# A fused state-space mixer and FFN on one core: seven of a unit's eight token chunks turned by VectorE in 32x32 squares and reordered through DRAM in place of TensorE, and scaled by GpSimd

## The chip, the core and the metric

The kernel runs on one core of a Trainium2 chip. The time is the device time of one execution in microseconds, and the median over several is given. The four engines that compute are TensorE (PE in the profile, with PEld for its weight loads), VectorE (DVE), ScalarE (ACT) and GpSimd (POOL). SyncE (SP) issues nearly all the transfers.

## What is computed

The input is x, two sequences of 512 tokens with 512 channels. A projection makes, for each token, a gate and a hidden vector (128 heads of 64), B and C (8 groups of 128) and one time step dt per head. Hidden, B and C go through a causal convolution of four taps and a SiLU. Then comes a chunked scan, chunks of 128 tokens:

```python
xch = (hs * dt[..., None]).reshape(b, nc, CHUNK, H, P)          # hidden scaled by the time steps
Y_diag = einsum('bzlhn,bzshn,bhzls,bzshp->bzlhp', Cc, Bc, L, xch)   # within a chunk
states = einsum('bzlhn,bhzl,bzlhp->bzhpn', Bc, decay_states, xch)   # carried to the next chunk
Y = Y_diag + Y_off + hs * D
g = y * silu(gate)                                                # then a group norm and the output projection
```

The result is added to x and normalised, and a linear layer with folded LoRA matrices, another addition and another normalisation follow.

## The kernel before

**Tiling.** The 128 heads are 16 units of 8 heads. A group g (0 to 7) has two units, e = 0 and 1. A unit's tokens are eight chunks c of 128 (the first four are one sequence, the last four the other). One pair (g, e, c) is a step; there are 128 of them. All engines run the same order of steps, unrolled in Python, and wait for one another by semaphores. The names below are those of the code.

**Hidden values, turned.** The projection leaves the hidden values of a unit in hs with channels on partitions and tokens along the free axis (four tiles j of 128 channels). The products of a chunk need the tokens on partitions, times dt: that is xdt, 128 tokens by 8 heads by 64. Before, `front` of TensorE (line 519) turns the four 128x128 pieces of a chunk into the PSUM bank p_hid (L526), and `front` of VectorE (line 1206) multiplies p_hid by the time steps in tok into xdt (L1210).

**A step on TensorE** has, in this order: the carried part of chunk c, one tile of the projection (L514 to L516), p_yd from xdt and the decay matrix (L690), `front` of the next chunk (p_hid, and for e = 0 also p_misc, L537 and L539), the state update p_st (L700 to L702, which waits for xd_ready; not for c = 3 and 7), the output projection of the chunk before (p_out, L562 to L564, which waits for g_hi and g_lo), and the rest of the step's projection tiles.

**Projection tiles** stand in a table by step. A step has one tile (both sequences, 24 matmuls) or two or three. In e = 0 the steps c = 0, 1, 6, 7 have more than one tile, in e = 1 the steps 0, 1, 5, 6, 7.

**A step on GpSimd** (`body`, line 1083) has, in this order: for c not 0 or 4, dh + eac (L1092); for c = 1, 2, 5, 6, state times elast (L1097); the low half of a weight tile two tiles ahead, w_lo (`split_lo`, L1034); the gating of y (`gate_y`, L1144, waits for y of VectorE); now and then a small rs (L1149); `skip` of the next chunk (L1063); `decay_hidden` of the next chunk (L1052, L1054, L1056), which makes xd, xd_hi and xd_lo from xdt and lets p_st go (not for c = 3 and 7); and, in a step with more tiles, a further w_lo for each. I call the first w_lo of a step its W1 and the second its W2.

**A step on SyncE** (line 463): eac of the next chunk (waits until dh + eac is done), a decay matrix (waits for p_yd), then the weights raw of the tiles four ahead. `load_w` waits for w_lo, since raw has two buffers: in a step with two tiles, the second raw is loaded when GpSimd has done W2.

**A step on VectorE** (line 1347): three convolution taps of a sequence, y = p_yd + dh (L1375), the state (L1383 or L1385), a tap, `front` (xdt, and for e = 0 cb, b_hi, b_lo), a tap, `mix` (decay times cb, L1227), a tap, the norm's sums, g_lo (L1251), `scale_off` (eac, L1258).

```python
def front(g, e, c):                       # VectorE
    dve.wait_ge(hid_ready, step(g, e, c) + 1)
    wait(dve, xd_scaled, carried(g, e, c))
    nc.vector.tensor_tensor(xdt[:], p_hid[:], bcast(tok[:, e, 1, c, :], 2, HD), ALU.mult).then_inc(xdt_ready, 1)
```

Of the kernel before, what the change touches and what calls it, by code (L numbers as in the profile page):

```python
# [22 lines left out]
P = 128  # L23
# [11 lines left out]
EPS = 1e-5  # L35
HALVES = (slice(0, HID // 2), slice(HID // 2, HID))
# [57 lines left out]
def mixer_ffn_kernel(nc, x_t, x_tok, w_t, unit_chan, group_chan, dt_bias, a_log, wo_t,  # L94
                     ffn_w, lora_a, lora_b, lora_w, ffn_bias, eye, upper, out):
    ctx = ExitStack()
    with ctx:
# [12 lines left out]
        elast_d = nc.dram_tensor("elast_d", (HEADS, CHUNKS), F32, kind="Internal").ap()  # L110
        tok_d = nc.dram_tensor("tok_d", (P, UNITS, 3 * CHUNKS * UH), F32, kind="Internal").ap()
# [16 lines left out]
        xdt = sb("xdt", [P, UH, HD])  # L128
        xd = sb("xd", [P, UH, HD])
# [51 lines left out]
        hid_ready, xdt_ready, xd_ready = sem("hid_ready"), sem("xdt_ready"), sem("xd_ready")  # L181
        cb_ready, cb_taken, bhi_ready = sem("cb_ready"), sem("cb_taken"), sem("bhi_ready")
# [74 lines left out]
        def decay_round(g, e, c):  # L257

            return 8 * g + (4 * e + c // 2 + 1) if c % 2 else 4 * g + (2 * e + c // 4 + 1)

# [119 lines left out]
        def _(sp):  # L380
            def load_w(g, t):
# [79 lines left out]
            sp.wait_ge(tok_here, 1)  # L461

            def body(g, last):
                for e in range(2):
                    for c in range(8):
# [34 lines left out]
        def _(pe):  # L500
# [528 lines left out]
        def _(pool):  # L1029
# [14 lines left out]

            def decay_hidden(g, e, c):
# [32 lines left out]
            pool.wait_ge(tok_here, 1)  # L1078
            decay_hidden(0, 0, 0)
# [3 lines left out]
            def body(g, last):  # L1083
                for e in range(2):
                    for c in range(8):
# [15 lines left out]
                        for i, t in enumerate(tiles):  # L1101
# [3 lines left out]
                            if i == 0 and (g, e, c) == (0, 0, 0):  # L1105
                                decay_hidden(0, 0, 1)
# [431 lines left out]
```

## Time and profile before

| | |
|---|---|
| median of 3 runs | 1598.37 us (1598.18 to 1598.73) |
| span of the profiled execution | 1596.2 us; what lies around the span, against the median, is 2.2 us |
| TensorE busy | 1577.7 us, 99% |
| VectorE busy | 1347.6 us, 84% |
| ScalarE busy | 1230.8 us, 77% |
| GpSimd busy | 1224.1 us, 77% |
| TensorE's granted clock | 9 (90% of full speed or more) in each of 40 slices |
| DMA | 178.69 MB, 34% of the 16 engines' span |

The profile is of one execution. The profiled execution's own time is its span, 1596.2 us, and the 2.2 us around it. Matmuls overlap in the records: a matmul lasts longer than the distance to the next, so what one costs is read from the distance between starts. PEld is the weight load, which overlaps too. "Idle before" is the engine's wait ahead of an instruction, with what ended it.

### The profile page before, as it was taken

The page shows a single profiled execution, that of the slowest core. Times are in us where ns is not written, and L with a number is a line of the kernel's source. Part 1 is how long each engine was busy: PE and PEld are TensorE (multiplying, and loading weights), DVE is VectorE, ACT ScalarE, POOL GpSimd, SP SyncE. Part 2 cuts the span into 40 slices and gives each one's busy share as a digit, 9 for nine tenths or more (in the row PEclk, how much of TensorE's full clock was granted, in tenths as well). Part 3 has the DMA queues.
Part 4 walks back from the last instruction along what each step waited for, and adds up shares of the span by engine and source line. Part 5 has one row for each costly group of instructions (what it writes and reads, how often), then busy time and mean ns, then how long its engine had stood idle before and what let it go on. Part 6 is the DMA issues. An engine that isn't in the chain of part 4 may idle for free.

```text
span 1596.2 us, 27397 instructions
## 1 busy us (share of the span) xinstructions
PE 1577.7 (99%) x9112; PEld 1299.6 (81%) x9112; DVE 1347.6 (84%) x1878; ACT 1230.8 (77%) x2391; POOL 1224.1 (77%) x1013
## 2 busy tenths in 40 slices
PE   8999999999999999999999999999999999999998
PEld 6878888888888888888888888888888888888865
DVE  6787898879979799787988889887998879978797
ACT  5888778886778877787877877878777886878864
POOL 4578788787797868878687787878688786787864
PEclk9999999999999999999999999999999999999999
DMA  3643424233242322333234332433334333342411
GB/s 116 200 157 108 130 83 153 87 115 108 87 145 96 123 100 100 129 100 109 87 115 140 99 123 74 131 118 92 116 101 136 102 102 106 100 149 77 142 60 60
DMA packets 88156, 178.69 MB, mean 112 GB/s; under 512 B 16592, under 2 KB 20688, under 8 KB 87760
## 3 DMA queue, kind: packets, MB, share of 16 engines
q1 hardware_dynamic: 87008, 176.77, 34.2%
q8 instruction: 74, 1.21, 0.3%
q14 instruction: 66, 0.54, 0.1%
q10 hardware_dynamic: 1008, 0.17, 0.1%
HBM read 172.17 MB, written 4.72 MB: 111 GB/s over the span
## 4 chain that ended last, share of the span: by engine, by line
PE 94%; DVE 1%; POOL 1%; ACT 1%; issue 1%; DMA 0%; SPq 0%; POOLq 0%; DVEq 0%; ACTq 0%
PE proj L514 16%; PE proj L516 16%; PE proj L515 16%; PE p_yd L690 8%; PE p_out L562 7%; PE p_out L564 7%; PE p_out L563 7%; PE p_st L571 5%; PE p_hid L526 4%; PE proj L626 2%; PE p_st L702 1%; PE p_st L700 1%; PE p_st L701 1%; PE p_misc L537 1%; PE p_misc L583 0%
## 5 line engine op out<-in xcount | busy, mean ns | idle before, releaser
L514 PE MATMUL proj<-x_hi,w_hi 128*128 128x512 f32 x1160 | 462.0, 398 | 7.6 <-DVE x_lo L1323 7.0
L515 PE MATMUL proj<-x_lo,w_hi 128*128 128x512 f32 x1160 | 452.9, 390 | 0.0
L516 PE MATMUL proj<-x_hi,w_lo 128*128 128x512 f32 x1160 | 452.9, 390 | 0.0
L1034 POOL TENSOR_TENSOR w_lo<-raw,w_hi 128x512 fp32r<-128x512 f32 x209 | 284.2, 1364 | 101.8 <-ACT w_hi L754 99.3
L1198 DVE SCALAR_TENSOR_TENSOR hs<-proj,uch,hs 128x511 f32<-128x511 f32 (+2 forms) x384 | 285.4, 743 | 42.4 <-ACT hs L781 37.5
L842 ACT ACTIVATE decay<-decay,tok 128x128 f32<-128x128 f32 x1024 | 312.4, 391 | 0.0
L514 PEld LDWEIGHTS proj<-x_hi,w_hi 128*128 128x128 f32 x1160 | 218.8, 189 | 53.2 <-issue 11.2
L516 PEld LDWEIGHTS proj<-x_hi,w_lo 128*128 128x128 f32 x1160 | 218.3, 188 | 46.2
L515 PEld LDWEIGHTS proj<-x_lo,w_hi 128*128 128x128 f32 x1160 | 218.9, 189 | 42.2
L1227 DVE TENSOR_TENSOR decay<-decay,cb 128x1024 f32<-128x1024 f32 x128 | 199.0, 1555 | 56.0 <-ACT decay L860 54.3
L1092 POOL TENSOR_TENSOR dh<-dh,eac 128x512 f32<-128x512 f32 x96 | 127.2, 1325 | 144.0 <-DVE eac L1258 140.3
L1144 POOL TENSOR_TENSOR y<-y,gate 128x512 f32<-128x512 f32 x128 | 180.0, 1406 | 50.3 <-DVE y L1375 50.3
L562 PE MATMUL p_out<-wo_hi,g_hi 128*128 128x512 f32 x512 | 203.6, 398 | 3.3 <-DVE g_lo L1251 3.3
L564 PE MATMUL p_out<-wo_hi,g_lo 128*128 128x512 f32 x512 | 200.1, 391 | 0.0
L563 PE MATMUL p_out<-wo_lo,g_hi 128*128 128x512 f32 x512 | 199.5, 390 | 0.0
L781 ACT ACTIVATE hs<-proj,uch 128x512 f32<-128x512 f32 x128 | 98.6, 773 | 78.8 <-PE proj L516 77.9
L980 ACT ACTIVATE ysq<-y 128x512 f32<-128x512 f32 x128 | 79.9, 624 | 98.8 <-POOL y L1144 98.8
L1375 DVE TENSOR_TENSOR y<-p_yd,dh 128x512 f32<-128x512 f32 x128 | 87.7, 685 | 68.7 <-PE p_yd L690 41.5
L1063 POOL TENSOR_TENSOR dh<-hs,uch 128x512 f32<-128x512 f32 x122 | 145.1, 1189 | 0.0
L754 ACT ACTIVATE w_hi<-raw 128x512 fp32r<-128x512 f32 x197 | 122.8, 623 | 28.2 <-PE proj L516 28.2
L1056 POOL TENSOR_TENSOR xd_lo<-xd,xd_hi 128x512 fp32r<-128x512 f32 x96 | 135.9, 1416 | 7.7
L690 PE MATMUL p_yd<-decay,xdt 128*64 128x128 f32 x2048 | 140.1, 279 | 0.0
(139 smaller groups left out, 3037.6 us busy)
## 6 DMA issues: line engine op xcount, KB each, us to landing
decay<-acum_d SPq DMA_DIRECT2D x128, 512.0 KB, 4.4
raw<-w_t SPq DMA_DIRECT2D x209, 256.0 KB, 2.9
eac<-eacum_d SPq DMA_DIRECT2D x192, 128.0 KB, 3.0
wo_raw<-wo_t SPq DMA_DIRECT2D x32, 256.0 KB, 4.0
c_new<-wo_t SPq DMA_DIRECT2D x32, 256.0 KB, 4.2
hs<-x_t SPq DMA_DIRECT2D x8, 256.0 KB, 5.7
acc<-x_tok SPq DMA_DIRECT2D x8, 256.0 KB, 3.1
out<-acc SPq DMA_DIRECT2D x8, 256.0 KB, 2.0
```

Of the source, the lines that this page charges most:

```text
L514: nc.tensor.matmul(dst[:], w_hi[:, ws, k, :], x_hi[:, k, cols], start=(k == 0), stop=False)
L515: nc.tensor.matmul(dst[:], w_hi[:, ws, k, :], x_lo[:, k, cols], start=False, stop=False)
L516: mm = nc.tensor.matmul(dst[:], w_lo[:, ws, k, :], x_hi[:, k, cols], start=False, stop=(k == KC - 1))
L562: nc.tensor.matmul(p_out[:], g_hi[:, j, :], wo_hi[:, j, :], start=(j == 0), stop=False)
L563: nc.tensor.matmul(p_out[:], g_hi[:, j, :], wo_lo[:, j, :], start=False, stop=False)
L564: mm = nc.tensor.matmul(p_out[:], g_lo[:, j, :], wo_hi[:, j, :], start=False, stop=(j == UT - 1))
L690: mm = nc.tensor.matmul(p_yd[(h % 2) * HD:(h % 2 + 1) * HD, h // 2, :], xdt[:, h, :], decay[:, dslot(c), h, :], start=True, stop=True)
L842: ins = nc.scalar.activation(decay[:, dslot(c), h, :], decay[:, dslot(c), h, :], ACT.Relu, scale=-1.0, bias=tok[:, e, 0, c, h:h + 1])
L1034: nc.gpsimd.tensor_tensor(w_lo[:, s].rearrange("p a b -> p (a b)"), raw[:, s, :], w_hi[:, s].rearrange("p a b -> p (a b)").bitcast(F32), A ...
L1144: nc.gpsimd.tensor_tensor(y[:], y[:], gate[:, c // CPB, :, (c % CPB) * P:(c % CPB + 1) * P], ALU.mult).then_inc(gated, 1)
L1198: nc.vector.scalar_tensor_tensor(out=dst[:, shift:], in0=src[:, :SEQ - shift], scalar=w, in1=dst[:, shift:], op0=ALU.mult, op1=ALU.add).th ...
L1227: nc.vector.tensor_tensor(decay[:, dslot(c)], decay[:, dslot(c)], bcast(cb[:, c, :], 1, UH), ALU.mult).then_inc(mix_ready, 1)
```

## The change

For the chunks c = 1 to 7 of every unit the turning leaves TensorE. Chunk 0 stays as it was. For the others:

1. VectorE's new `turn_blocks` transposes a chunk's hidden values in 32x32 squares, hs to x_blk (one instruction, 128x512). It does so two chunks ahead, in the place where `front` had multiplied.
2. SyncE's `store_blocks` writes x_blk to DRAM (turned_d), one transfer of 256 KB; `load_blocks`, behind the weights of the step, waits until that has landed and reads it back in four transfers of 64 KB, each to 32 partitions in runs of 512 bytes, to x_tok_sb. Now tokens lie on partitions.
3. GpSimd's `scale_tokens` multiplies x_tok_sb by dt_blk into xdt, behind W1 and ahead of `gate_y`, when x_here says that the four reads have landed and p_yd of the running chunk is done. `lay_dt` copies a unit's time steps to dt_blk, two small copies per unit.

The scratch for GpSimd's own DMA descriptors is made smaller to leave room for the new tiles; GpSimd issues no transfers.

```diff
@@ SyncE
+            def store_blocks(g, e, c):
+                n = turn_n(g, e, c)
+                sp.wait_ge(blocks_turned, n)
+                wait(sp, x_here, 64 * (n - 2))
+                sp.dma_start(turned_d[n % 2].rearrange("i a n -> (i a) n"),
+                             x_blk[:].rearrange("p q j b -> p (q j b)")).then_inc(blocks_stored, 16)
+            def load_blocks(g, e, c):
+                n = turn_n(g, e, c)
+                sp.wait_ge(blocks_stored, 16 * n)
+                wait(sp, x_here, 64 * (n - 1))
+                wait(sp, xdt_ready, step(g, e, c) - 1)
+                for q in range(UT):
+                    sp.dma_start(x_tok_sb[q * BLK:(q + 1) * BLK, n % 2].rearrange("a i j b -> a i (j b)"),
+                                 turned_d[n % 2, :, :, q * P:(q + 1) * P].rearrange("i a n -> a i n")).then_inc(x_here, 16)
...
+                        o2, e2, c2 = ahead(e, c, 2)
+                        if c2 and not (last and o2):
+                            store_blocks(g + o2, e2, c2)
                         for t in tiles_of(e, c, last):
                             off, n = divmod(t.n + 4, GRP_TILES)
                             if not (last and off):
                                 load_tile(g + off, LOOP_TILES[n], last)
+                        if c2 and not (last and o2):
+                            load_blocks(g + o2, e2, c2)
@@ TensorE, front
-                wait(pe, xdt_ready, step(g, e, c))
-                if c == 0 or c == CPB:
-                    pe.wait_ge(hs_ready, 8 * u + (8 if c else 7 if u else 4))
-                for j in range(UT):
-                    mm = nc.tensor.transpose(p_hid[:, 2 * j:2 * j + 2, :].rearrange("p a b -> p (a b)"),
-                                             hs[:, e, j, c * P:(c + 1) * P], ident[:])
-                mm.then_inc(hid_ready, 1)
+                if c == 0:
...
@@ GpSimd
+            def scale_tokens(g, e, c):
+                pool.wait_ge(x_here, 64 * turn_n(g, e, c))
+                pool.wait_ge(yd_ready, step(g, e, c))
+                if c == 1:
+                    pool.wait_ge(dt_blk_ready, 2 * (2 * g + e + 1))
+                nc.gpsimd.tensor_tensor(xdt[:].rearrange("p h d -> p (h d)").rearrange("p (j i b) -> p i j b", j=UT, i=UT),
+                                        x_tok_sb[:, turn_n(g, e, c) % 2], bcast(dt_blk[:, c], 3, BLK), ALU.mult).then_inc(xdt_ready, 1)
...
                             elif i == 0:
+                                if c < 7:
+                                    scale_tokens(g, e, c + 1)
                                 gate_y(g, e, c)
@@ VectorE
+            def turn_blocks(g, e, c):
+                u = 2 * g + e
+                wait(dve, blocks_stored, 16 * (turn_n(g, e, c) - 1))
+                dve.wait_ge(hs_ready, 8 * u + (8 if c >= CPB else 7 if u else 4))
+                nc.vector.transpose(x_blk[:], hs[:, e, :, c * P:(c + 1) * P].rearrange("p j (q a) -> p q j a", q=UT)
+                                    ).then_inc(blocks_turned, 1)
...
                         if more:
                             front(g + off, ne, ncn)
+                        o2, e2, c2 = ahead(e, c, 2)
+                        if c2 and not (last and o2):
+                            turn_blocks(g + o2, e2, c2)
```

GpSimd's rows from the end of step (e = 1, c = 7) of a group through step (e = 0, c = 0) of the next, before:

```order
L1034 TENSOR_TENSOR w_lo<-raw,w_hi 128x512 x2
L1144 TENSOR_TENSOR y<-y,gate 128x512
L1149 TENSOR_TENSOR rs<-var,minus_half 128x1
L1063 TENSOR_TENSOR dh<-hs,uch 128x512
L1052 TENSOR_TENSOR xd<-xdt,tok 128x512
L1054 CAST xd_hi<-xd 128x512
L1056 TENSOR_TENSOR xd_lo<-xd,xd_hi 128x512
L1034 TENSOR_TENSOR w_lo<-raw,w_hi 128x512
```

and the same place after the change, where the first w_lo is W2 of step 7, the second W1 of step 0 and the last W2 of step 0:

```order
L1069 TENSOR_TENSOR w_lo<-raw,w_hi 128x512
L1087 COPY dt_blk<-tok 128x16x4
L1087 COPY dt_blk<-tok 128x16x4
L1069 TENSOR_TENSOR w_lo<-raw,w_hi 128x512
L1095 TENSOR_TENSOR xdt<-x_tok_sb,dt_blk 128x4x4x32
L1205 TENSOR_TENSOR y<-y,gate 128x512
L1210 TENSOR_TENSOR rs<-var,minus_half 128x1
L1116 TENSOR_TENSOR dh<-hs,uch 128x512
L1105 TENSOR_TENSOR xd<-xdt,tok 128x512
L1107 CAST xd_hi<-xd 128x512
L1109 TENSOR_TENSOR xd_lo<-xd,xd_hi 128x512
L1069 TENSOR_TENSOR w_lo<-raw,w_hi 128x512
```

The scaling now stands between W1 and the gating, ahead of all else that the step makes. SyncE's rows from step (e = 0, c = 7) to the first of step (e = 1, c = 1), before:

```order
L366 DMA decay<-acum_d 128x1024
L388 DMA raw<-w_t 128x512 x2
L355 DMA uch<-unit_chan 128x28
L345 DMA tok<-tok_d 128x192
L351 DMA elast<-elast_d 128x64
L374 DMA eac<-eacum_d 64x512 x2
L366 DMA decay<-acum_d 128x1024
L388 DMA raw<-w_t 128x512 x2
L374 DMA eac<-eacum_d 64x512 x2
```

and after:

```order
L376 DMA decay<-acum_d 128x1024
L396 DMA turned_d<-x_blk 128x512
L416 DMA raw<-w_t 128x512 x2
L406 DMA x_tok_sb<-turned_d 32x4x128 x4
L365 DMA uch<-unit_chan 128x28
L355 DMA tok<-tok_d 128x192
L361 DMA elast<-elast_d 128x64
L384 DMA eac<-eacum_d 64x512 x2
L376 DMA decay<-acum_d 128x1024
L396 DMA turned_d<-x_blk 128x512
L416 DMA raw<-w_t 128x512 x2
L406 DMA x_tok_sb<-turned_d 32x4x128 x4
```

The four reads of x_tok_sb stand behind the second raw, and so behind the wait for W2 that raw has.

## Rows read from the trace of the kernel before

**Rows 1.** The page, busy time, share of the span and instructions of engines.

```profile
PE 1577.7 (99%) x9112; PEld 1299.6 (81%) x9112; DVE 1347.6 (84%) x1878; ACT 1230.8 (77%) x2391; POOL 1224.1 (77%) x1013
```

**Rows 2.** The page, the chain of work that ended last, shares by line.

```profile
PE proj L514 16%; PE proj L516 16%; PE proj L515 16%; PE p_yd L690 8%; PE p_out L562 7%; PE p_out L564 7%; PE p_out L563 7%; PE p_st L571 5%; PE p_hid L526 4%; PE proj L626 2%; PE p_st L702 1%; PE p_st L700 1%; PE p_st L701 1%; PE p_misc L537 1%; PE p_misc L583 0%
```

**Rows 3.** Timeline of TensorE, start and length, behind two p_yd (e = 0, e = 1).

```profile
709.91 0.66 PE L526 MATMUL p_hid<-ident,hs 128*128 128x128 f32 x4
710.41 0.39 PE L537 MATMUL p_misc<-cT,bT 128*128 128x128 f32 x2
710.55 0.47 PE L700 MATMUL p_st<-xd_hi,b_hi 128*128 128x512 f32 x1
...
730.32 1.09 PE L690 MATMUL p_yd<-decay,xdt 128*64 128x128 f32 x16
731.35 0.66 PE L526 MATMUL p_hid<-ident,hs 128*128 128x128 f32 x4
731.76 0.48 PE L700 MATMUL p_st<-xd_hi,b_hi 128*128 128x512 f32 x1
```

**Rows 4.** Groups by line: count, busy us, mean ns, idle before and its releasers.

```profile
L1052 POOL TENSOR_TENSOR xd<-xdt,tok 128x512 f32<-128x512 f32 x96 | 135.0, 1406 | 0.6 <-DVE xdt L1210 0.6
L1210 DVE TENSOR_TENSOR xdt<-p_hid,tok 128x512 f32<-128x512 f32 x128 | 87.1, 680 | 0.0
```

**Rows 5.** The tile xdt: shortest, median and longest ns, first and last start.

```profile
L1052 POOL TENSOR_TENSOR xd<-xdt,tok x96: 1036/1087/2047, 65.1 to 1550.1; 128x512 f32<-128x512 f32 x96
```

**Rows 6.** Timeline of GpSimd, (e = 1, c = 7) into the next group's first step.

```profile
831.05 2.52 POOL L1034 TENSOR_TENSOR w_lo<-raw,w_hi 128x512 fp32r<-128x512 f32 x2
833.53 1.29 POOL L1144 TENSOR_TENSOR y<-y,gate 128x512 f32<-128x512 f32 x1
...
838.98 1.29 POOL L1056 TENSOR_TENSOR xd_lo<-xd,xd_hi 128x512 fp32r<-128x512 f32 x1
```

**Rows 7.** Timeline of SyncE's queue, start and length of issues.

```profile
832.39 0.33 SPq L388 DMA_DIRECT2D raw<-w_t  x1
...
843.24 1.09 SPq L374 DMA_DIRECT2D eac<-eacum_d  x2
```

**Rows 8.** DMA issues: count, KB each, median us from issue to landing.

```profile
eac<-eacum_d SPq DMA_DIRECT2D x192, 128.0 KB, 3.0
...
tok<-tok_d SPq DMA_DIRECT2D x14, 96.0 KB, 2.6
```

**Rows 9.** Timeline of TensorE, first step of a group and the second step's update.

```profile
830.74 1.09 PE L690 MATMUL p_yd<-decay,xdt 128*64 128x128 f32 x16
...
844.35 0.48 PE L700 MATMUL p_st<-xd_hi,b_hi 128*128 128x512 f32 x1
```

**Rows 10.** Timeline of GpSimd at other steps: (0,1) into (0,2), (0,6), (1,0).

```profile
649.72 1.66 POOL L1034 TENSOR_TENSOR w_lo<-raw,w_hi 128x512 fp32r<-128x512 f32 x1
...
657.70 1.30 POOL L1144 TENSOR_TENSOR y<-y,gate 128x512 f32<-128x512 f32 x1 [1.89 <-DVE y L1375]
...
663.26 1.69 POOL L1056 TENSOR_TENSOR xd_lo<-xd,xd_hi 128x512 fp32r<-128x512 f32 x1
...
707.86 1.31 POOL L1056 TENSOR_TENSOR xd_lo<-xd,xd_hi 128x512 fp32r<-128x512 f32 x1
...
730.96 2.54 POOL L1034 TENSOR_TENSOR w_lo<-raw,w_hi 128x512 fp32r<-128x512 f32 x2
...
738.38 1.30 POOL L1056 TENSOR_TENSOR xd_lo<-xd,xd_hi 128x512 fp32r<-128x512 f32 x1
```

**Rows 11.** Timeline of TensorE, state updates of steps (0,2) and (1,1).

```profile
668.07 0.47 PE L700 MATMUL p_st<-xd_hi,b_hi 128*128 128x512 f32 x1
...
743.15 0.48 PE L700 MATMUL p_st<-xd_hi,b_hi 128*128 128x512 f32 x1
```

More of the change, by code:

```diff
@@ L110, in mixer_ffn_kernel @@
         elast_d = nc.dram_tensor("elast_d", (HEADS, CHUNKS), F32, kind="Internal").ap()
+        turned_d = nc.dram_tensor("turned_d", (2, UT, BLK, UT * P), F32, kind="Internal").ap()
         tok_d = nc.dram_tensor("tok_d", (P, UNITS, 3 * CHUNKS * UH), F32, kind="Internal").ap()
@@ L128, in mixer_ffn_kernel @@
         xdt = sb("xdt", [P, UH, HD])
+        x_blk = sb("x_blk", [P, UT, UT, BLK])
+        x_tok_sb = sb("x_tok_sb", [P, 2, UT, UT, BLK])
+        dt_blk = sb("dt_blk", [P, CHUNKS, UT, UT])
         xd = sb("xd", [P, UH, HD])
@@ L461, in _ @@
             sp.wait_ge(tok_here, 1)
+            store_blocks(0, 0, 1)
+            load_blocks(0, 0, 1)
             def body(g, last):
@@ L521, in front @@
                 u = 2 * g + e
-                wait(pe, xdt_ready, step(g, e, c))
-                if c == 0 or c == CPB:
-                    pe.wait_ge(hs_ready, 8 * u + (8 if c else 7 if u else 4))
-                for j in range(UT):
-                    mm = nc.tensor.transpose(p_hid[:, 2 * j:2 * j + 2, :].rearrange("p a b -> p (a b)"),
-                                             hs[:, e, j, c * P:(c + 1) * P], ident[:])
-                mm.then_inc(hid_ready, 1)
+                if c == 0:
+                    wait(pe, xdt_ready, step(g, e, c))
+                    pe.wait_ge(hs_ready, 8 * u + (7 if u else 4))
+                    for j in range(UT):
+                        mm = nc.tensor.transpose(p_hid[:, 2 * j:2 * j + 2, :].rearrange("p a b -> p (a b)"),
+                                                 hs[:, e, j, c * P:(c + 1) * P], ident[:])
+                    mm.then_inc(hid_ready, 1)
                 if e == 0:
@@ L1043, in split_both, with lay_dt @@
                 split_lo(g, t)
+            def lay_dt(u):
+                g, e = u // 2, u % 2
+                if g:
+                    pool.wait_ge(unit_loaded[e], 48 * g + 32)
+                wait(pool, xdt_ready, 8 * u)
+                for r in range(2):
+                    nc.gpsimd.tensor_copy(dt_blk[:, :, r::2, :], tok[:, e, 1].rearrange("p c (j q) -> p c q j", j=UT)).then_inc(dt_blk_ready, 1)
+            def scale_tokens(g, e, c):
[5 more added lines that the diff above has]
+                                        x_tok_sb[:, turn_n(g, e, c) % 2], bcast(dt_blk[:, c], 3, BLK), ALU.mult).then_inc(xdt_ready, 1)
             def decay_hidden(g, e, c):
@@ L1117, in body @@
                         if not tiles:
[L1118 removed]
+                            if c < 7:
+                                scale_tokens(g, e, c + 1)
+                            else:
                                 lagged_rms(g, e, c)
@@ L1126, in body @@
                                     skip(g + off, ne, ncn)
+                        if c == 7 and not (last and off):
+                            lay_dt(2 * g + e + 1)
                         if last and e == 1 and c >= 5:
@@ L1206, in front @@
             def front(g, e, c):
-                dve.wait_ge(hid_ready, step(g, e, c) + 1)
-                wait(dve, xd_scaled, carried(g, e, c))
-                nc.vector.tensor_tensor(xdt[:], p_hid[:], bcast(tok[:, e, 1, c, :], 2, HD), ALU.mult).then_inc(xdt_ready, 1)
+                if c == 0:
+                    dve.wait_ge(hid_ready, 2 * g + e + 1)
+                    wait(dve, xd_scaled, carried(g, e, c))
+                    nc.vector.tensor_tensor(xdt[:], p_hid[:], bcast(tok[:, e, 1, c, :], 2, HD), ALU.mult).then_inc(xdt_ready, 1)
                 if e == 0:
```

10 lines of the change are left out of this document (8 added, 2 removed).

## The prediction

> **What bounds the kernel now.** I read the page's busy times first: TensorE is busy 99% of the span, GpSimd 77%, VectorE 84% [rows 1]. The chain that ended last says the same: nearly all of it is TensorE's own lines, and p_hid, the turning, has 4% [rows 2]. So a matmul that leaves shortens the kernel, as long as the other engines still deliver before TensorE asks. The second reading is therefore how early they deliver. In the timeline I set the end of GpSimd's xd_lo, which is what the state update p_st waits for, against the start of p_st:
>
> - chunk 1 of e = 0: 838.98 + 1.29 = 840.27 against 844.35, slack 4.1 [rows 6, 9];
> - chunk 1 of e = 1: 739.68 against 743.15, slack 3.5 [rows 10, 11];
> - chunk 2 of e = 0: 664.95 against 668.07, slack 3.1 [rows 10, 11];
> - chunk 6 of e = 0: 709.17 against 710.55, slack 1.4 [rows 3, 10].
>
> These are margins of 1.4 to 4.1 us in steps of some 12 (1596.2/128). GpSimd idles 23% on average, but not there.
>
> **What TensorE gives back.** p_hid to the next matmul is 710.41 - 709.91 = 0.50 us for e = 0 and 731.76 - 731.35 = 0.41 for e = 1 [rows 3]; I take it that what follows p_yd now starts where p_hid did. 56 chunks of each kind leave: 56 x 0.50 + 56 x 0.41 = 51.0 us. The floor is 1598.4 - 51.0 = 1547.4.
>
> The Trainium skill (TensorE: Matmul & The Clock Gate, Part 4) gives about 275 ns for a transpose on TensorE within a kernel. By that 448 of them would be 123 us and the time 1475. The rows decide against it: the records last that long, but they start 0.10 to 0.125 us apart, so the 51.0 stands.
>
> **VectorE.** 112 products of 0.68 us leave [rows 4] and 112 transposes of the same 512 elements per partition come, in the same place. No row has such a transpose. Bounds: the 0.68 of the product, and twice that; I take 0.68 as the same element count, so nothing. Twice would add 0.7 us to steps in which VectorE is nearly full, at most 112 x 0.7 = 76 us if all showed; I reckon a quarter, 19.
>
> **GpSimd** gets 112 products. Nearest row: xd<-xdt,tok, also 512 elements with a broadcast operand, 1036 ns at the shortest, 1406 in the mean, 2047 at the longest [rows 4, 5]. I take 1.2. Its load goes from 1224 to 1224 + 134 = 1358 us, 85% of the old span: it still fits on average. dt_blk's 32 small copies I cost at nothing: they stand where GpSimd waits for ScalarE or a step's first weights.
>
> The spread from 1036 to 2047 for one instruction shows contention [rows 5]. The Trainium skill (SBUF — State Buffer, two separate sides) says that GpSimd and a VectorE operation with two SBUF inputs exclude each other at a shared port pair for the whole instruction. It speaks against the change, since p_hid lay in PSUM and the new product reads and writes SBUF only. By it the longest value would be common, and 112 x (2.05 - 1.2) = 95 us more GpSimd time would result; the mean in the rows above lies far nearer the short end.
>
> **The round trip through DRAM.** The reads of x_tok_sb stand in SyncE's queue behind the second raw of a step, and that waits for GpSimd's W2 (in the rows: W2 ends at 831.05 + 1.26 = 832.31, raw is issued at 832.39) [rows 6, 7]. From the end of W2: raw 0.35, four issues at about 0.5 each (two eac took 1.09 [rows 7]), of which three lie ahead of the last one's start, and the last one's landing. For that the neighbours are 2.6 (96 KB) and 3.0 (128 KB) [rows 8]; I take 2.75. T = 0.35 + 1.5 + 2.75 = 4.6 us. Bounds: 3.9 (issues of 0.33, landing 2.6) and 5.3 (issues of 0.55, landing 3.3 behind raw's own 256 KB). In steps with one tile nothing holds the reads: turned some 5 us behind p_yd, stored (up to 3.0) and read (4.3), they land some 12 us behind p_yd, and the product wants them 13 behind it or later. There I cost the trip at nothing; its cover is about 1 us.
>
> With two tiles there is a loop: W2 of step c-1, T, the product for c+1 in step c, then gating, skip, decay_hidden, W2 of step c, and again T. Behind the product in GpSimd's queue stand the gating (which ScalarE's squares and g_hi and VectorE's g_lo wait for) and decay_hidden (which p_st waits for).
>
> **Chunk 1 of e = 0.** Product from 832.31 + 4.6 = 836.9, gating from 838.1 in place of 833.53: 4.6 late [rows 6]. The slack is 4.1, and TensorE arrives 2 x 0.50 earlier. p_st waits 4.6 - 4.1 + 1.0 = 1.5 us.
>
> **Chunk 1 of e = 1.** W2 ends at 730.96 + 1.27 = 732.2, the product starts at 736.8, the gating at 738.0 in place of 733.5: 4.5 late; with the slack of 3.5 and 2 x 0.41: 1.9 us [rows 10, 11].
>
> **Chunk 2 of e = 0.** W2 of step 0 ended at 649.72 + 1.66 = 651.38, the gating began 6.3 later, after a wait of 1.89 for y [rows 10]. Now W2 is 4.6 late, the gating can follow 4.6 + 1.2 = 5.8 behind it: 4.1 late in all. Slack 3.1; TensorE has gained 3 x 0.50 and lost 1.5: 1.0 us. I add 1.0 for chunk 4, to which the lateness passes by the squares and eac on VectorE; this is an estimate from chunk 2's.
>
> **Chunk 6 of e = 0 and chunk 4 of e = 1**, the tight ones in plain steps: slack 1.4, product 1.04 (part of it in a wait for y), TensorE 1.0 earlier: 0.7 us each. I read the second's slack as 6's.
>
> **The start.** The first product has no earlier unit to hide under, and pays store and read: 3 us more, an estimate from T.
>
> **The sum.** Waits: 8 x 1.5 + 8 x 1.9 + 8 x (1.0 + 1.0) + 15 x 0.7 + 3 = 12 + 15.2 + 16 + 10.5 + 3 = 56.7. Against 51.0: +5.7. The profiled execution, 1596.2 + 2.2 around it, is the median's 1598.4; so 1604.
>
> **Rivals.**
> *The round trip is shorter or better hidden: faster.* For: with T = 3.9 each of the four looped places (chunks 1, 1, 2, 4) loses about 0.7 of its wait, 8 x 4 x 0.7 = 22: 1582. Should the product fall into waits for y in the tight steps, as one of 1.89 us shows [rows 10], another 10 go: 1572. It decides where T is below about 4.4 (5.7/32 = 0.2 under my value). Against: four issues with a raw of 256 KB ahead of them. Chance 0.28 for 1555 to 1595.
> *All is hidden.* 1547. For: GpSimd has 372 us of idle time [rows 1]. Against: the slacks above. 0.08.
> *The trip or contention is worse.* T = 5.3: +22, 1626; twice the transpose: +19, 1623; both 1645. For: VectorE and GpSimd would both be near 90% in H steps. 0.30 for above 1614.
> *It only changes places, as forecast:* waits of p_st for xd_lo eat what TensorE gave back, 1595 to 1614. 0.34.
> That the change doesn't take p_hid off TensorE is excluded by the order of its instructions.
>
> **How the numbers follow.** 1604 is the forecast of the likeliest case. Two runs of this kernel differ by up to 0.03%, and about 0.2% (3.2 us) is what a measurement can tell from no change. Faster by over that: 0.08 + 0.28; of the likeliest case's 0.34, 0.12 lies within 0.2% of 1598.4 and 0.22 above it; so slower is 0.22 + 0.30 = 0.52. The range leaves out full success and the sum of all the bad bounds: 1565 to 1640. The likeliest case's own range is 1595 to 1614.
>
> **What would show it.** TensorE: 64 p_hid instead of 512, its busy time some 50 us lower, and its idle time up from 18 to some 75 us, the largest part "p_st waits for GpSimd's xd_lo" with 1 to 2 us at chunks 1 of both units, little at chunks 3 and 7. GpSimd: a wait ahead of the product, released by the DMA to x_tok_sb, of 3 us in steps (0,0) and (1,0), under 1 in one-tile steps. x_tok_sb from W2's end to landing: 4.6. VectorE: the transpose at 0.6 to 0.7, its idle time unchanged. The product at 1.0 to 1.4. The prediction is wrong if x_tok_sb lands within 3.5 us of W2, if the product waits in one-tile steps as well (the cover of 1 us is thin: 0.5 us in each of the 8 such steps of a group would be 30 us), if the transpose takes over 1 us, or if waits move to p_yd or p_out through g_lo.

## The result and the profile after

The changed kernel takes 1672.19 us (median of 4 runs, 1671.84 to 1673.55) against 1598.46 of the kernel before on the same chip: ratio 1.0464, interval 1.045 to 1.0479. It is 73.7 us slower. The forecast had 1604, range 1565 to 1640.

The page of the changed kernel: busy times, then the chain that ended last by engine, then some groups of instructions (busy, mean ns | idle before, releaser), then the new transfers (KB each, us to landing).

```profile
PE 1567.9 (94%) x8664; PEld 1268.2 (76%) x8664; DVE 1380.4 (83%) x1878; ACT 1230.5 (74%) x2391; POOL 1376.6 (82%) x1157
...
POOL 31%; PE 21%; issue 19%; DVE 16%; ACT 8%; DMA 2%; SPq 2%; ACTq 0%; DVEq 0%; POOLq 0%
...
L1015 ACT ACTIVATE ysq<-y 128x512 f32<-128x512 f32 x128 | 80.6, 630 | 221.0 <-POOL y L1205 220.9
...
L1095 POOL TENSOR_TENSOR xdt<-x_tok_sb,dt_blk 128x512 f32<-128x512 f32 x112 | 123.1, 1099 | 61.8 <-DMA x_tok_sb<-turned_d 61.8
...
turned_d<-x_blk SPq DMA_DIRECT2D x112, 256.0 KB, 2.5
x_tok_sb<-turned_d SPq DMA_DIRECT2D x448, 64.0 KB, 2.1
```

Against [rows 1]: TensorE does 448 matmuls less, yet its busy time falls by only 9.8 us (1577.7 to 1567.9), and span less busy time grows from 18.5 to 103.8. The chain, nearly all TensorE before [rows 2], now runs a third over GpSimd. The granted clock, its mean over the span:

```profile
core 0: 1671.7 us, clock 0.986
```

It was 0.999 in the run before; 0.013 of 1671.7 is 21.7 us.

What TensorE waits for, in the view of waits (us in total, times, longest). Before, this view had 0.4 us of p_st for xd_lo, 0.6 of proj for "issue", and none for var.

```profile
PE p_st L735 <- POOL xd_lo L1109: 31.7, 30, 2.2
PE p_misc L572 <- DVE var L1309: 20.1, 12, 2.3
PE proj L549 <- issue: 15.2, 18, 1.9
PE proj L549 <- DVE x_lo L1393: 6.9, 1, 6.9
PE p_hid L561 <- ACT hs L828: 4.5, 5, 1.5
PE p_out L597 <- issue: 4.4, 7, 0.8
PE p_st L735 <- DVE eac L1328: 3.4, 1, 3.4
```

**One trip, followed.** GpSimd's timeline from the end of step (0,7) to step (1,1) of a group (start, length, [idle before]):

```profile
961.14 1.74 POOL L1069 TENSOR_TENSOR w_lo<-raw,w_hi 128x512 fp32r<-128x512 f32 x1
962.83 0.41 POOL L1087 COPY dt_blk<-tok 128x64 f32<-128x64 f32 x2
963.20 1.29 POOL L1069 TENSOR_TENSOR w_lo<-raw,w_hi 128x512 fp32r<-128x512 f32 x1
967.04 1.74 POOL L1095 TENSOR_TENSOR xdt<-x_tok_sb,dt_blk 128x512 f32<-128x512 f32 x1 [2.55 <-DMA x_tok_sb<-turned_d]
968.75 1.28 POOL L1205 TENSOR_TENSOR y<-y,gate 128x512 f32<-128x512 f32 x1
...
972.84 1.59 POOL L1109 TENSOR_TENSOR xd_lo<-xd,xd_hi 128x512 fp32r<-128x512 f32 x1
974.40 1.72 POOL L1069 TENSOR_TENSOR w_lo<-raw,w_hi 128x512 fp32r<-128x512 f32 x1
976.08 1.75 POOL L1146 TENSOR_TENSOR dh<-dh,eac 128x512 f32<-128x512 f32 x1
977.78 1.51 POOL L1151 TENSOR_TENSOR state<-state,elast 128x512 f32<-128x512 f32 x1
979.25 1.72 POOL L1069 TENSOR_TENSOR w_lo<-raw,w_hi 128x512 fp32r<-128x512 f32 x1
```

SyncE's queue at the same place:

```profile
962.95 0.33 SPq L416 DMA_DIRECT2D raw<-w_t  x1
963.39 1.79 SPq L406 DMA_DIRECT2D x_tok_sb<-turned_d  x4
```

And TensorE's timeline:

```profile
971.68 1.09 PE L725 MATMUL p_yd<-decay,xdt 128*64 128x128 f32 x16
974.49 0.50 PE L735 MATMUL p_st<-xd_hi,b_hi 128*128 128x512 f32 x1 [1.71 <-POOL xd_lo L1109]
...
976.22 0.47 PE L549 MATMUL proj<-x_hi,w_hi 128*128 128x512 f32 x1 [0.77 <-issue]
976.52 0.39 PE L550 MATMUL proj<-x_lo,w_hi 128*128 128x512 f32 x1
...
981.07 0.65 PE L549 MATMUL proj<-x_hi,w_hi 128*128 128x512 f32 x1 [1.85 <-issue]
981.52 0.63 PE L550 MATMUL proj<-x_lo,w_hi 128*128 128x512 f32 x1
981.94 0.63 PE L551 MATMUL proj<-x_hi,w_lo 128*128 128x512 f32 x1
```

W2 of step 7 ends at 962.88 (961.14 + 1.74), and the second raw and the four reads are issued at once; only when the last has landed can the product start, at 967.04, 4.2 later. The gating follows at 968.75, 5.9 behind W2's end, where before it followed 1.2 behind [rows 6]. TensorE then waits three times: for xd_lo (1.71), for the low half w_lo that is ready at 976.12 (0.77), and for the next at 980.97 (1.85). The view calls the last two "issue", since the wait lies at the weight load; both end 0.10 behind GpSimd's w_lo, as do all of this name at this step. Behind the third gap matmuls of 512 columns start 0.43 apart, not 0.23. The granted clock of that stretch (windows: us, TensorE busy, matmuls, granted clock, DMA share, GB/s):

```profile
976.00:980.00 4.00, 3.00 (x12) 1.00 0.51 132
980.00:984.00 4.00, 2.93 (x7) 0.65 0.85 261
984.00:988.00 4.00, 4.00 (x18) 0.92 0.20 70
```

So TensorE fell from its upper level (2.4 GHz) to the lower (1.2 GHz) for some 3.4 us (by these shares from 981.2 to 984.6), in which eight matmuls took 0.2 us more each, 1.6 in all.

Not every fall costs that. The profiled execution has this step in seven groups with such waits. In two the fall came behind the third gap, and the step took 25.8 us. In three it came ahead of the third gap, which shrank from 1.85 to 0.28, 0.28 and 1.00, and the step took 24.2. In two there was no fall, though the third gap was 1.88 and 1.85, and the step took 23.6 and 24.4. A fall ahead of a wait was paid by the wait.

**The other late chain** is at the step (0,1) of a group, on VectorE:

```profile
878.25 1.11 DVE L1497 TENSOR_REDUCE sqs<-ysq 128x128 f32<-128x512 f32 x1 [2.84 <-ACT ysq L1015]
879.28 1.34 DVE L1321 TENSOR_TENSOR g_lo<-y,g_hi 128x512 fp32r<-128x512 f32 x1
...
881.74 1.24 DVE L1315 SCALAR_TENSOR_TENSOR wo_lo<-wo_raw,uch,wo_hi 128x512 fp32r<-128x512 f32 x1
882.90 0.15 DVE L1309 TENSOR_SCALAR var<-p_misc 128x1 f32<-128x1 f32 x1
```

and TensorE at the same place:

```profile
879.79 1.09 PE L725 MATMUL p_yd<-decay,xdt 128*64 128x128 f32 x16
883.20 0.46 PE L572 MATMUL p_misc<-cT,bT 128*128 128x128 f32 x2 [2.31 <-DVE var L1309]
```

The late gating makes the squares (ysq) late; VectorE stands idle 2.84 us before its sum of them; var, which it reads out of p_misc, stands behind that; and `front` of TensorE may not write p_misc before.

### The profile page after: what moved, and what is told of

It reads as the page before. It is cut to its first block, busy times and chain, and to the rows that moved or that the text cites. A ratio compares the mean times of both kernels' runs of the same rounds, so it can differ in the third digit from the quotient of the medians.

```text
span 1671.7 us, 27534 instructions
## 1 busy us (share of the span) xinstructions
PE 1567.9 (94%) x8664; PEld 1268.2 (76%) x8664; DVE 1380.4 (83%) x1878; ACT 1230.5 (74%) x2391; POOL 1376.6 (82%) x1157
## 4 chain that ended last, share of the span: by engine, by line
POOL 31%; PE 21%; issue 19%; DVE 16%; ACT 8%; DMA 2%; SPq 2%; ACTq 0%; DVEq 0%; POOLq 0%
POOL y L1205 7%; DVE hs L1259 5%; PE proj L549 5%; PE proj L550 5%; PE proj L551 5%; POOL w_lo L1069 4%; POOL xd L1105 4%; POOL dh L1116 3%; POOL xd_lo L1109 3%; POOL xdt L1095 3%; POOL dh L1146 2%; DVE g_lo L1321 2%; ACT decay L877 2%; POOL xd_hi L1107 2%; DMA x_tok_sb<-turned_d 2%
## 5 line engine op out<-in xcount | busy, mean ns | idle before, releaser
L549 PE MATMUL proj<-x_hi,w_hi 128*128 128x512 f32 x1160 | 467.1, 403 | 22.1 <-issue 15.2
L1069 POOL TENSOR_TENSOR w_lo<-raw,w_hi 128x512 fp32r<-128x512 f32 x209 | 293.1, 1404 | 36.2 <-ACT w_hi L789 31.4
L549 PEld LDWEIGHTS proj<-x_hi,w_hi 128*128 128x128 f32 x1160 | 221.4, 191 | 73.7 <-issue 30.7
L1146 POOL TENSOR_TENSOR dh<-dh,eac 128x512 f32<-128x512 f32 x96 | 131.1, 1366 | 111.1 <-DVE eac L1328 111.0
L597 PE MATMUL p_out<-wo_hi,g_hi 128*128 128x512 f32 x512 | 208.0, 406 | 9.2 <-issue 4.4
L1205 POOL TENSOR_TENSOR y<-y,gate 128x512 f32<-128x512 f32 x128 | 194.9, 1522 | 11.0 <-DVE y L1446 11.0
L1095 POOL TENSOR_TENSOR xdt<-x_tok_sb,dt_blk 128x512 f32<-128x512 f32 x112 | 123.1, 1099 | 61.8 <-DMA x_tok_sb<-turned_d 61.8
L1116 POOL TENSOR_TENSOR dh<-hs,uch 128x512 f32<-128x512 f32 x122 | 155.8, 1277 | 0.0
```

The lines of the kernel that those rows point to most:

```text
L549: nc.tensor.matmul(dst[:], w_hi[:, ws, k, :], x_hi[:, k, cols], start=(k == 0), stop=False)
L597: nc.tensor.matmul(p_out[:], g_hi[:, j, :], wo_hi[:, j, :], start=(j == 0), stop=False)
L1069: nc.gpsimd.tensor_tensor(w_lo[:, s].rearrange("p a b -> p (a b)"), raw[:, s, :], w_hi[:, s].rearrange("p a b -> p (a b)").bitcast(F32), A ...
L1116: nc.gpsimd.tensor_tensor(dh[:], hs[:, e, :, c * P:(c + 1) * P], bcast(d_skip(e), 2, P), ALU.mult).then_inc(dskip_done if c % CPB else dh_ ...
L1205: nc.gpsimd.tensor_tensor(y[:], y[:], gate[:, c // CPB, :, (c % CPB) * P:(c % CPB + 1) * P], ALU.mult).then_inc(gated, 1)
```

## The experiments

All are 4 runs each beside the kernel before on the same chip (1598.0 to 1598.4). "Idle" is span less TensorE's busy time: 18.5 us before, 103.8 in the changed kernel. Step times are medians over the groups of p_yd to p_yd, from starts in the timeline. Where a run lies outside the ranges that were expected of it, the text says so.

**e1: TensorE's turning taken away, nothing put in.** The kernel before; TensorE turns chunk 0 alone, VectorE multiplies an old p_hid.

```diff
-                wait(pe, xdt_ready, step(g, e, c))
-                ... four transposes, every chunk
+                if c == 0:
+                    ... wait and four transposes
-                dve.wait_ge(hid_ready, step(g, e, c) + 1)
+                dve.wait_ge(hid_ready, 2 * g + e + 1)
```

> The kernel before, in which TensorE turns only chunk 0 of a unit; for chunks 1 to 7 VectorE multiplies what chunk 0 left in p_hid, so the turning of seven chunks is left out and nothing takes its place. It shows what the removal gives by itself. Both theories (GpSimd's added work is what costs; the wait for the round trip through DRAM is what costs) need about the same: the sum of the steps that kept their pace in the changed kernel says 0.40 us for each of 112 chunks, 45 us, so 1553; by the 0.41 and 0.50 of the prediction 1547. Above 1565 the removal itself opens gaps, and part of the miss would be there.

Measured 1587.99 (ratio 0.994, 0.9923 to 0.9956), 23 us above the 1565 from which the removal itself opens gaps. Its busy times and two of TensorE's waits:

```profile
PE 1541.0 (97%) x8664; PEld 1256.1 (79%) x8664; DVE 1348.5 (85%) x1878; ACT 1228.1 (77%) x2391; POOL 1225.3 (77%) x1013
...
PE p_st L700 <- DVE eac L1258: 7.8, 9, 1.2
...
PE p_misc L537 <- DVE var L1239: 5.9, 6, 1.0
```

Busy 1541.0 is 36.7 less than before, not 51; idle is 44.7, 26 more. Steps such as (0,2) shorten by 0.39 (11.63 to 11.23), but (0,1) grows by 0.6, (0,6) by 0.65 and (1,4) by 0.7, with waits for VectorE's eac, var and state. **With the other engines' work as it was, 10 us were to be had.**

**e2: the changed kernel without store and load**, a constant in x_tok_sb, so the seven chunks' values are left out.

```diff
-                            store_blocks(g + o2, e2, c2)
...
-                            load_blocks(g + o2, e2, c2)
...
-                pool.wait_ge(x_here, 64 * turn_n(g, e, c))
```

> The changed kernel without store_blocks and load_blocks: VectorE still transposes, GpSimd still multiplies, but a constant tile that is filled once, and it waits only for p_yd of the chunk before. Left out: the real hidden values of seven chunks. If GpSimd's added work (112 products of 1.1 us, ahead of the gating, and what queues behind them) costs the time, it stays slow: 1625 to 1660. If the wait for the round trip (61.8 us ahead of the products in all) and what it shifts costs it, this comes close to the removal alone: 1555 to 1580. In between, both.

**e3: the load put behind the first raw of a step with several tiles**, everything else as changed.

```diff
-                        for t in tiles_of(e, c, last):
+                        for i, t in enumerate(tiles_of(e, c, last)):
+                            if i == 1 and c2 and not (last and o2):
+                                load_blocks(g + o2, e2, c2)
...
-                        if c2 and not (last and o2):
+                        if len(tiles_of(e, c, last)) < 2 and c2 and not (last and o2):
                             load_blocks(g + o2, e2, c2)
```

> The changed kernel with one move on SyncE: in steps with two or three tiles the four reads of x_tok_sb are issued behind the first weights' transfer, no longer behind the second, which waits for GpSimd's second w_lo. Theory of the round trip: the waits of 2.5 us at chunk 0 and about 1 at chunk 1 vanish and with them most of the loss, 1600 to 1625. Theory of GpSimd's work: at most 62 us of waits go and the work moves up into them, but the queue stays full in these steps, 1640 to 1665.

e2: 1611.80 (1.0084, 1.0069 to 1.0099), between its two ranges, so both causes count. e3: 1615.58 (1.0113, 1.0098 to 1.0128), in the range of the round trip. The profile of e3, busy times and GpSimd's wait for the trip:

```profile
PE 1551.6 (96%) x8664; PEld 1259.8 (78%) x8664; DVE 1393.7 (86%) x1878; ACT 1227.7 (76%) x2391; POOL 1380.3 (85%) x1157
...
POOL xdt L1097 <- DMA x_tok_sb<-turned_d: 7.2, 3, 4.0
```

One move of the load takes GpSimd's wait from 61.8 to 7.2 us and the time down by 56.6. What the transfers cost otherwise, contention for the DMA engines too, is within e3 less e2: 3.8 us.

**e4: the kernel before with an unused product of 128x512 on GpSimd** at the change's place, 112 times (smaller descriptor scratch, to make room).

```diff
+                                if c < 7:
+                                    scale_tokens(g, e, c + 1)     # x_tok_sb times dt_blk, to an unused tile
                                 gate_y(g, e, c)
```

> The kernel before with one thing added: GpSimd's product of 128x512, from and to tiles that nobody else uses, at the place where the change puts it (behind the first w_lo of a step, ahead of the gating, 112 times, behind p_yd of the chunk before). TensorE keeps its turning and VectorE its product. Theory of GpSimd's work: the time rises by 30 to 70 us, to 1630 to 1670, with waits of TensorE at steps (1,1), (0,1) and (1,7). Theory of the round trip: under 15 us, below 1613.

1621.90 (1.0149, 1.0134 to 1.0165), clock 1.0, between its two ranges: 23.8 us over the kernel before. 10 of them are idle (28.8). The other 13 are TensorE's busy time; half of them, 6.4 us, lies within p_out, whose matmuls start 0.233 apart in place of 0.227. In e2, e3, e12 and the changed kernel, which have the same product, they start 0.227 apart, so these 6.4 us can't be put down to the product alone; the cause of the 13 stays open. What this run shows of the product is the 10 us of idle time.

**e5: e2 with the product on VectorE; e6: e3 with the product on VectorE; e7: the changed kernel with the product behind the gating; e8: e3 with it there.**

```diff
e5, e6, front of VectorE
+                else:
...
+                    nc.vector.tensor_tensor(xdt[:]..., x_tok_sb[:, turn_n(g, e, c) % 2], bcast(dt_blk[:, c], 3, BLK), ALU.mult)
e7, e8, GpSimd
-                                if c < 7:
-                                    scale_tokens(g, e, c + 1)
                                 gate_y(g, e, c)
+                                if c < 7:
+                                    scale_tokens(g, e, c + 1)
```

> This is e2 (no store, no load, a constant in x_tok_sb) with the product by the time steps moved back to VectorE, at the place that its product has in the kernel before: GpSimd's work is again that of the kernel before but for the laying out of the time steps, and VectorE has the turn in squares (0.70 us, 112 times) beside its product. It leaves out the values of the seven chunks. Theory A, GpSimd's 123 us of products are what stands between e2 and e1 (1611.8 and 1588.0): 1588 to 1594, with POOL y again waiting for VectorE some 40 to 50 us in sum. Theory B, VectorE's 79 us of turning cost it (VectorE holds y, the variance and g_lo back): 1604 to 1616, no better than e2.

> This is e3 (in steps with more than one tile the load of the turned blocks stands behind the first weight load) with the product on VectorE as in e5; it computes everything. If what is left of the trip is hidden (in e3 the blocks land before their use almost everywhere) and GpSimd's products are the other half, it lies within 4 us of e5, 1588 to 1598, perhaps ahead of the kernel before. If the trip still comes late in some steps, VectorE waits for x_tok_sb at the head of its queue, and y and the squares with it: 1610 to 1630, no better than e3's 1615.6. If VectorE's added work decides, e5 and e6 both stand at 1604 to 1616.

> This is the changed kernel with one difference in GpSimd's order: the product stands behind the gating of y rather than ahead of it. The load is as late as in the changed kernel. If the wait for the round trip does its harm through the queue, because the gating stands behind it and with it the squares, the variance and p_misc, then the waits of p_misc for the variance at (0,1) and (1,7) (some 20 us in all) and the late ysq go, while xd_lo comes no later, since the product now fills the time that the trip takes: 1640 to 1655. If instead xd_lo and w_lo are what TensorE waits for and the gating's own wait for y is merely put ahead of them, it is unchanged or slower: 1668 to 1690.

> This is e3 with the product behind the gating of y: early load, later product. If e3's remaining loss of some 17 us over the kernel before is the gating held back by the product (1.1 us of GpSimd's time ahead of it in each step), it gains 5 to 15 us: 1600 to 1611. If it is GpSimd's sum of work, or xd_lo and w_lo at the end of its step, the order does not matter or hurts: 1613 to 1630.

e5: 1621.10 (1.0144, 1.0126 to 1.0161). e6: 1625.54 (1.0174, 1.0157 to 1.0191). e7: 1655.44 (1.0359, 1.0344 to 1.0375). e8: 1631.44 (1.0208, 1.0193 to 1.0223). Theory A of e5 was wrong, relieving GpSimd cost 9 us more than it gave, and e5 lies above theory B's range too. e6 falls in the range of a trip that still comes late, but not for that reason: VectorE waits for x_tok_sb once, 6.4 us. e7 and e8 are 0.4 and 1.4 us over the ranges whose side they take. A part of e5's loss is the product's length on VectorE; in the tile's view (shortest/median/longest ns) the same 512 elements from SBUF and from PSUM:

```profile
L1259 DVE TENSOR_TENSOR xdt<-x_tok_sb,dt_blk x112: 680/1207/1847, 70.4 to 1584.3; 128x512 f32<-128x512 f32 x112
L1253 DVE TENSOR_TENSOR xdt<-p_hid,tok x16: 678/680/682, 63.8 to 1506.7; 128x512 f32<-128x512 f32 x16
```

e7 bore the queue out: with the same late load, the gating freed from the product is worth 16.8 us; (1,7) falls from 13.51 to 11.69 and (0,1) from 16.76 to 15.66, and p_misc waits 11.3 us for var in place of 20.1. With the early load (e8 against e3) the same move costs 15.9, by later xd_lo at (1,4) and later eac at (1,5). So the product belongs ahead of the gating once its data are there in time.

**e9: e3 with the laying out of the time steps in step (e,0); e10: e9 with squares for ten of sixteen chunks only.**

```diff
e9, scale_tokens
                 if c == 1:
+                    if (g, e) != (0, 0):
+                        lay_dt(2 * g + e)
...
-                        if c == 7 and not (last and off):
-                            lay_dt(2 * g + e + 1)
e10
+IN_SQUARES = ((1, 3, 4, 5, 6), (1, 3, 4, 6, 7))
...
```

> This is e3 with GpSimd's laying out of the time steps (two copies, once a unit) moved from step (e,7) to step (e,0), just ahead of the first product of the unit; it computes everything. If these copies are what keeps the variance back at the end of a unit, the step (1,7) falls from e3's 11.73 us towards e1's 10.28 and the kernel by up to 10 us, to 1605 to 1610. If the delay at (1,7) is the products ahead of it in the queue, it stays at 11.7 and the kernel at 1612 to 1618.

> This is e9 with TensorE turning chunks 0, 2, 7 of the first unit and 0, 2, 5 of the second unit of a pair of units, and the squares the other ten: GpSimd then has no product in steps (0,1), (0,6), (1,1) and (1,4), where e3 lost. It computes everything. If the loss is made by the product in those steps, they come back to what e1 shows and the kernel to 1588 to 1596, level with or just ahead of the kernel before (1598). If VectorE, GpSimd and ScalarE are behind over a whole unit, and those steps are only where TensorE meets them, the waits appear again there or one step on, and the time is 1600 to 1612.

e9: 1627.04 (1.018, 1.0165 to 1.0195), its (1,7) unchanged at 11.73: the copies were not the cause. But it is 11.5 us slower than e3, above both ranges. Of the 7.1 us between the two profiled executions 5.2 are at (1,1), where the last gap is now 1.86 or 1.87 in all of groups 1 to 6, and the granted clock falls behind five of them, against three in e3. e10: 1621.69 (1.0148, 1.0133 to 1.0164), above both ranges as well. Both hopes fell. In e10 the waits moved on, to (1,5) (10.7 us for eac). That fits engines which are behind over the whole unit, but isn't shown: in the step before, VectorE has a product and a turn, as it has throughout e11 below, whose (1,5) is as long (15.38 for 15.40; 13.92 in e3).

**e11: e1 with VectorE's turn alone; e12: e2 without it, GpSimd's product alone.** With e1 and e2 they make a table.

```diff
e11, VectorE
+                        if c2 and not (last and o2):
+                            turn_blocks(g + o2, e2, c2)      # result unused
e12, VectorE: the same lines taken away
```

> This is e1 (TensorE turns chunk 0 alone, VectorE's product as before from an old p_hid) with VectorE's turn in squares added at the changed kernel's place, its result unused; nothing is stored or loaded, GpSimd is untouched. It leaves out the right values of seven chunks. It prices VectorE's 0.70 us, 112 times, by itself on e1's 1588.0. Theory A, VectorE has room: 1588 to 1592. Theory B, VectorE sets TensorE's pace at (0,1), (0,6) and (1,7): 1598 to 1615, and then most of e5's 1621 is VectorE's.

> This is e2 (no store, no load, constant in x_tok_sb) without VectorE's turn in squares: GpSimd has its 112 products and the laying out of the time steps, VectorE 76 us less than in the kernel before. It leaves out the values of seven chunks. With e1, e2 and e11 it makes a table of both engines' added work. Theory A, GpSimd's product costs what it adds: 1605 to 1612, nearly e2. Theory B, each engine's work alone is nearly hidden and only both together cost: 1588 to 1597.

| | time | idle | clock |
|---|---|---|---|
| e1, neither | 1587.99 | 44.7 | 0.999 |
| e11, VectorE's turn (and its product) | 1608.98 | 65.1 | 0.999 |
| e12, GpSimd's product | 1623.81 | 65.1 | 0.992 |
| e2, both (VectorE's product gone) | 1611.80 | 62.2 | 0.999 |

Ratios to before: e11 1.0068 (1.0053 to 1.0083), in theory B's range; e12 1.0157 (1.0141 to 1.0174), above both of its ranges. Either engine's added work makes TensorE idle 20 us more, and both together no more than one. e5 is e11 with the product's inputs in SBUF and the laying out on GpSimd: VectorE is busy 39 us more and the time 12.1 longer. But e12, with 80 us less work on VectorE than e2, is 12.0 us slower at nearly the same idle time. Their timelines at the step (1,1) differ by 0.2 us of a gap: 1.65 to 1.67 us in e2 and no fall of the clock behind any of the six; 1.85 to 1.88 in e12, and a fall behind five of six. In e3 both occur: 1.66 or 1.67 three times without, 1.85 or 1.86 three times with a fall. (The expectation of e14 puts a fall in every pair of units; it was five.) These are single executions: e2's profiled one has the clock of the table, its others 0.996 to 0.999, e12's 0.992 to 0.996. e12 itself prices a fall: the step took 21.98 us in the group without one and 23.54 to 23.59 in the five with, so 1.6 each, 8 in all. The longer gap at the same clock makes it 21.98 for 21.55, 0.4 each. e2, timeline and window (us, busy time and count of TensorE, PEld, VectorE, ScalarE and GpSimd, granted clock, DMA share, GB/s):

```profile
751.39 0.47 PE L543 MATMUL proj<-x_hi,w_hi 128*128 128x512 f32 x1 [1.67 <-issue]
...
752.00:756.00 4.00, 4.00 (x19) 3.30 (x18) 4.00 (x5) 1.64 (x3) 4.00 (x4) 1.00 0.36 126
```

e12:

```profile
756.13 0.47 PE L543 MATMUL proj<-x_hi,w_hi 128*128 128x512 f32 x1 [1.86 <-issue]
...
757.14 0.60 PE L544 MATMUL proj<-x_lo,w_hi 128*128 128x512 f32 x1
757.53 0.63 PE L545 MATMUL proj<-x_hi,w_lo 128*128 128x512 f32 x1
...
756.00:760.00 4.00, 3.87 (x11) 3.17 (x12) 2.17 (x3) 0.71 (x2) 4.00 (x4) 0.64 0.51 176
```

**e13, e14: the gaps of step (1,1) filled** in the changed kernel and in e12, with 84 unused matmuls into p_hid.

```diff
+                        if (e, c) == (1, 1) and not last:
+                            fill(4)                        # ahead of p_st
...
+                                if e == 1 and not last:
+                                    fill(4)                # ahead of each projection behind p_st
                                 project(g, t)
```

> This is the changed kernel with unused matmuls of 512 columns (0.23 us each at full clock) on TensorE in step (1,1): four ahead of the state update p_st and four ahead of each projection tile that follows it, where TensorE waits 1.7, 0.8 and 1.9 us in the changed kernel; it computes everything. Theory A, the fall of the granted clock behind these gaps is a cost of its own: where it fell at (1,1) the projections that follow go at full clock again, the granted clock of the run rises from 0.986 to 0.989 or more, and the time falls by 5 to 15 us, to 1657 to 1667. Theory B, the gaps alone are the cost, and the matmuls only take time: 1672 to 1690, as the filling cannot fit exactly.

> This is e12 (GpSimd's product alone, no trip, no turns; 1623.8 us, granted clock 0.992, a fall of the clock behind the gap of step (1,1) in every pair of units) with the same unused matmuls as e13. It leaves out the values of seven chunks. Theory A: the falls at (1,1) go, the granted clock is 0.998 or more, the step (1,1) goes from 23.5 us to the 21.6 of e2, and the time to 1609 to 1615, which is e2's, so that e12 and e2 differ by the clock alone. Theory B: the falls stay or the filling costs what it saves, 1622 to 1632, and the 12 us between e12 and e2 have another cause.

e13: 1667.76 (1.0435, 1.0419 to 1.0451), clock 0.991, 0.8 us over theory A's range. e14: 1617.31 (1.0116, 1.0099 to 1.0133), clock 0.997, between its two ranges; the step (1,1) goes from 23.54 to 22.01, without a fall in any group that was filled. The page of e14:

```profile
PE 1565.0 (97%) x8748; PEld 1273.9 (79%) x8748; DVE 1318.6 (82%) x1766; ACT 1226.1 (76%) x2391; POOL 1387.0 (86%) x1158
```

**More work, less time:** 84 matmuls of 0.23 us, 19 us of TensorE's time, and the kernels are 4.4 and 6.5 us faster. The falls behind these gaps are a cost of their own. e14 is what shows it: by steps, 7.0 us of the profiled execution's gain are at (1,1). e13 is weaker: only 3.5 us of its profiled gain are at (1,1), 3.8 are at (0,4), which was not filled, and the other steps lose on balance. e14 stays 5.5 over e2, so I can't say that the clock explains all 12.0, but it explains at least 6.5.

## Why the prediction was wrong, by its steps

It said slower as the likelier sign, and the wait for the trip that it named is the largest part; the size missed the range by 32 us, and most of the path from that wait to TensorE was another. By steps of one run to the next: before 1598.2, turning gone -10.2 (e1), both engines' work +23.8 (e2), transfers with an early load +3.8 (e3), the load behind the second raw +56.6 (after). In the profiled execution idle rose by 85.3 and busy time fell by 9.8, 75.5 in sum; the forecast had 56.7 and 51.0, 5.7 in sum. So 28.6 of the miss are in the waits and 41.2 in what TensorE gave back.

**Right.** *The trip.* From W2's end to the product in (0,0) and (1,0) it took 4.1 to 5.7 us, 4.2 in the median of 15, against T = 4.6; the pieces were raw 0.33, four issues 1.79 in all (0.45 each for 0.5) and a median landing of 2.1 for 2.75. GpSimd's wait of 61.8 lies as forecast at (0,0) and (1,0), 43.6 of it, 2.7 a time for 3; but it also waited 0.6 a time in a one-tile step, (0,2), hardly in the others, and 1.1 a time at (1,6) in seven groups. The prediction had named waits in one-tile steps as a sign against it.

*The transpose* took 0.70 for 0.68, *the product* 1.10 for 1.2 (1042 ns at the shortest, 1052 in the median, 2058 at the longest). The Trainium skill (SBUF — State Buffer, two separate sides) has GpSimd and a VectorE operation with two SBUF inputs exclude each other at a shared port pair; that did not make the longest value common on GpSimd, and what there is of it shows on VectorE's side, in e5. The prediction's bound for a doubled transpose, 112 x 0.7, is 78 and not 76, which changes nothing.

*Four of the six places where p_st was to wait*, summed from TensorE's idle rows by step: (1,1) 14.9 for 15.2 (11.5 for xd_lo in seven groups, 3.4 for eac in the last), (0,4) 7.4 for 8, (0,6) and (1,4) together 10.5 for 10.5. How well these sums agree is in part luck: the 8 of (0,4) was carried over from chunk 2, where nothing came of it, and in e1, without any trip or product, p_st at (0,6) waits 6.9 all the same, for eac.

**Wrong, the waits: 56.7 forecast, 85.3 measured.** The step that failed is "T, then p_st": I followed the lateness only to xd_lo, which is 31.7 of the 85.3. But all that stands behind the product in GpSimd's queue is late by as much. At (0,1) p_st was to wait 1.5 us a time, 12 in all; it waited 2.2 in all, since TensorE was stopped ahead of it in `front`, by var: 8.6 there and 11.4 at (1,7). At (0,2), where 8 were forecast, p_st never waited for xd_lo, since TensorE came later from (0,1). At (1,1) the projections waited 13.8 for w_lo, on top of p_st. p_hid waited 4.5 at (1,7) for hs. The prediction named p_yd and p_out through g_lo as places that would prove it wrong; it did not look at p_misc, though the gating's lateness was in its sum.

**Wrong, what TensorE gives back: 51.0 forecast.** The term is too large, and it is not what the time gets. Steps without a wait shorten by 0.37 to 0.41 in e1, 112 x 0.39 = 44; its busy time falls by 36.7 and its time by 10.2 only, since VectorE's and GpSimd's chain was as near as TensorE's. The slacks of 1.4 to 4.1 us were read at four places; at (0,1) p_misc for var and at (0,6) p_st for eac, which set much of e1, I had read none. So the floor of 1547 and the rival "all is hidden" were never there: 1588 is what is left with no new work at all. And the rival of a shorter trip (1555 to 1595) had no room either: with no trip whatever, e2 takes 1611.8.

**Wrong, left out: the clock.** Busy time fell by 9.8 where e1's fell by 36.7: 26.9 us of longer matmuls, 21.7 of them by the mean granted clock (0.986 for 0.999). The lower level came behind gaps, and the work that followed paid. e14 shows that it can be a cost of its own. The 21.7 are worked out from the clock and are busy time; what they cost directly is less, since at (1,1) three of the five falls were paid by shorter waits. e13 got back 4.4; the rest of the clock's share is not shown by a run.

**The rivals.** "The trip or contention is worse" (1623 to 1645) had the right sign and the wrong reason: T was 4.2 and not 5.3, and the transpose was not doubled. "GpSimd's load still fits on average" (85% forecast) was right as a sum and beside the point: in e4 the product alone makes TensorE idle 10 us more. Of the 152.5 us that GpSimd's busy time rose, 123.1 are the products, 6.6 the laying out and 23 its other instructions on balance (the gating alone is 14.9 longer, and xd_hi 22.6 shorter).

The other idea, that a lighter load on one engine would bring the time back, fell in e5, e6, e10 and e12. No version of this change beat the kernel before; the best that computes everything, e3, stays 17 us above it.

## What to carry to other kernels

Where one engine is busy 99% and three others 77 to 84% in one loop of waits, taking work off the first can show the next bound at once: take the work out alone and measure (10 us of 51 here) before paying for its replacement. When an instruction in an in-order queue gets a new wait, list everything behind it and who waits for each (here xd_lo, w_lo and, through squares and var, p_misc), not only its own result. A load whose data are ready goes ahead of a transfer that waits for a busy engine; that one move was worth 57 us.

## What the runs showed of the hardware that I had not expected

At one place of the program, (1,1), the granted clock of TensorE fell to 1.2 GHz behind gaps of 1.85 to 1.88 us in eight cases of nine in e3 and e12 and in five of six in e9, and stayed at 2.4 GHz behind the nine of 1.65 to 1.67 (e2, e3). The length of the last gap does not settle it alone: in the changed kernel, where two more gaps stand ahead, it fell behind two of four such gaps. The Trainium skill (TensorE: Matmul & The Clock Gate, Part 1) says that idleness brings the lower level; the rows agree in kind. 19 us of useless matmuls in such gaps made a kernel 6.5 us faster (e12 to e14). And a VectorE product of 512 elements, 680 ns with an input in PSUM, took 1207 ns in the median with both inputs in SBUF; all but one of the 112 overlapped an instruction of GpSimd, and that one took 681 (e5).
